# Fused cross-attention and mixture-of-experts block: the mixed context tile's probabilities move to a buffer of their own, and its text part and the denominators' passes are cut so that a step has at most one of them

## What is computed

```python
ctx_img = context[:, :IMG_LEN]      # 257 rows
ctx_txt = context[:, IMG_LEN:]      # 1344 rows
q = rms_norm(linear(x, q_w, q_b), norm_q_w).reshape(B, L, NH, HD)      # L = 512, NH = 16, HD = 32
...
scores = jnp.einsum('bqhd,bkhd->bhqk', q, k) * scale
probs = jax.nn.softmax(scores, axis=-1)
return jnp.einsum('bhqk,bkhd->bqhd', probs, v)
...
img_x = attention(q, k_img, v_img)
txt_x = attention(q, k, v)
out = (txt_x + img_x).reshape(B, L, DIM)
return linear(out, o_w, o_b)
```

## Time and profile before

| | |
|---|---|
| median of 3 runs | 1184.51 us (1183.47 to 1185.18) |
| profiled execution, its own time | 1186.64 us |
| its span in the trace | 1184.9 us |
| granted TensorE clock over the span | 0.996 of full speed |
| busy: TensorE, VectorE, ScalarE, GpSimd | 1113.4, 856.5, 651.0, 201.1 us |
| exponentials (L720), 384 plain ones | 372.3 us, mean 1022 ns |
| additions (L977), 64 and 62 | 146.6 and 142.0 us, mean 2291 and 2290 ns |

### The profile page before, as it was taken

How to read it: one execution, slowest core, us unless ns; L and a number is a source line. 1 busy time by engine, 2 the same in 40 slices (tenths; PEclk the granted TensorE clock), 3 DMA queues, 4 the chain that set the end, 5 groups by cost and what they waited for, 6 DMA issues and landing times. The chain is left out here.

```text
span 1184.9 us, 21824 instructions
## 1 busy us (share of the span) xinstructions
PE 1113.4 (94%) x8948; PEld 414.9 (35%) x8948; DVE 856.5 (72%) x1058; ACT 651.0 (55%) x916; POOL 201.1 (17%) x307
## 2 busy tenths in 40 slices
PE   6899999999999999999998999888999999999996
PEld 2342222344222344422233432222544444333332
DVE  6677889898889988788898878997878942222221
ACT  5558998444999744599964469885221121221221
POOL 1220000143000024300002440001110021333442
PEclk9999999999999999999999999999999999999998
DMA  8852000777300086910009583013823329999742
GB/s 299 193 116 45 2 2 11 165 156 195 74 2 2 11 208 135 207 38 2 2 22 228 134 191 112 2 37 109 343 80 116 116 76 338 357 314 314 220 63 33
DMA packets 142859, 150.15 MB, mean 127 GB/s; under 512 B 108832, under 2 KB 109088, under 8 KB 137760
## 3 DMA queue, kind: packets, MB, share of 16 engines
q1 hardware_dynamic: 135328, 131.57, 38.5%
q0 software_dynamic: 5120, 10.82, 4.7%
q10 hardware_dynamic: 2304, 6.29, 2.1%
HBM read 101.96 MB, written 21.51 MB: 104 GB/s over the span
## 5 line engine op out<-in xcount | busy, mean ns | idle before, releaser
L720 ACT ACTIVATE work<-ps 128x1024 f32<-128x1024 f32 x384 | 372.3, 1022 | 31.3 <-PE ps L1216 15.0
L1222 PE MATMUL ps<-work,vals 128*32 128x512 f32 (+2 forms) x1664 | 220.3, 600 | 3.8 <-DVE nums L965 2.1
L1073 PE MATMUL ps<-wts,work 128*128 128x512 f16 x864 | 194.7, 379 | 11.2 <-DVE work L779 10.9
L1216 PE MATMUL ps<-quer,keys 32*128 32x512 f16 x2496 | 171.9, 377 | 22.7 <-ACT work L720 15.5
L977 DVE TENSOR_TENSOR work<-work 128x2048 f32<-128x2048 f32 x64 | 146.6, 2291 | 6.2 <-ACT work L720 0.5
L977 DVE TENSOR_TENSOR attn<-attn,work 128x2048 f32<-128x2048 f32 x62 | 142.0, 2290 | 5.1
L1073 PEld LDWEIGHTS ps<-wts,work 128*128 128x128 f16 x864 | 83.0, 98 | 118.6 <-issue 19.0
L1878 DVE COPY xgt<-ps 128x320 f32<-128x320 f32 x32 | 15.7, 491 | 137.3 <-PE ps L2046 137.3
L2055 PE MATMUL ps<-wring,xgt 128*80 128x512 f32 x256 | 114.9, 592 | 0.0
L1073 PE MATMUL ps<-wts,hl 128*128 128x512 f16 x432 | 100.5, 384 | 12.9 <-DVE wts L761 7.5
L535 POOL TENSOR_SCALAR small<-small 128x1 f32<-128x1 f32 x68 | 20.1, 295 | 540.2 <-ACT work L630 540.2
(11 more groups left out here) (224 smaller groups left out, 1399.2 us busy)
## 6 DMA issues: line engine op xcount, KB each, us to landing
wring<-in_wx SPq DMA_DIRECT2D x32, 1536.0 KB, 8.5
raw<-in_ctx SPq DMA_DIRECT2D x52, 256.0 KB, 3.2
rb<-sums_inverse ACTq DMA_DIRECT2D x48, 128.0 KB, 4.0
work<-in_x SPq DMA_DIRECT2D x8, 512.0 KB, 4.4
table<-nums SPq DMA_DIRECT2D x16, 256.0 KB, 2.5
work<-in_x SPq DMA_DIRECT2D x12, 256.0 KB, 3.1
x<-work SPq DMA_DIRECT2D x12, 256.0 KB, 2.7
x2t_rows<-nums SPq DMA_DIRECT2D x12, 256.0 KB, 2.6
```

Source lines behind the costliest of these rows:

```text
L720: act.activation(prob[0:rows, s % PROBS, 2 * half:2 * half + 2, :], ps[0:rows, 2 * pair:2 * pair + 2, :], ACT.Exp, scale=SCALE, bias=pad i ...
L1073: mm = pe.matmul(out, lhs(a, c)[:, cols], wts[:, w, z, c * D:(c + 1) * D], start=(k == 0), stop=(k == len(steps) - 1))
L1216: mm = pe.matmul(ps[:, 2 * pair + h % 2, :], k[h * HD:(h + 1) * HD, :], q[h * HD:(h + 1) * HD, :], start=(e == 0), stop=(e == len(terms) - 1))
L1222: return pe.matmul(ps[h * HD:(h + 1) * HD, NUM, :], vals[a:z, ORDER[n], g * P + h * HD:g * P + (h + 1) * HD], prob[a:z, s % PROBS, h, :], ...
```

## The change

The probabilities of the mixed tile get a buffer of their own, `mixp`, 8 KB a partition at the place of `raw`, `hl0` and `rcp`, which rest during attention. The ring `prob` then holds only the 12 other tiles of a group: `place(g, n)` numbers them, `used` gives the count of `a_av` at which a tile's last reader is done, and `chances` picks the buffer. The exponentials of tile 2 wait for the mixed pieces of the group before. In the first group of batches 1 to 3 they wait for `f_chk` instead, because `rcp` lies in the new buffer. The exponentials of n = 3 now wait for the addition of n = 11, those of n = 4 for that of n = 12, and those of n = 5 and 6 for the image sum.

`mixed_text` becomes four pieces of 128 columns at n = 3, 4, 5 and 6 (`MIXED_AT`), `text_part` moves to n = 2, 7, 8 and 9 (`TEXT_AT`), and the image's four pieces become three of 172, 172 and 168 columns at n = 10, 11 and 12 (`image_third`, `IMAGE_CUT`). `first_loads` waits for the last mixed piece of the batch and stands later in SyncE's order, VectorE converts the next batch's first tile after the additions of n = 9 and 10 instead of 6 and 7, and GpSimd's copies into `sel` (which shares the place of `raw`) wait for the last mixed piece too.

```diff
-IMAGE_AT = [5, 10, 11, 12]
+IMAGE_AT = [10, 11, 12]
+IMAGE_CUT = [0, 172, 344, L]
+MIXED_AT = [3, 4, 5, 6]
+TEXT_AT = [2, 7, 8, 9]
...
+        self.mixp = at("mixp", 194 * KB_, [P, 4, L], F32)
...
+        def place(g, n):
+
+            return g * (KT - 1) + (n if n < 2 else n - 1)
+
+        def used(bb, g, n):
+
+            return bb * NG * (KT - 1) + place(g, n) + 1
+
+        def chances(g, n):
+
+            return m.mixp if n == 2 else prob[:, place(g, n) % PROBS, :, :]
...
             def first_loads(bb, b):
-                sp.wait_ge(c_lo, kvn(bb - 1, KT - 2))
+                sp.wait_ge(a_av, used(bb - 1, NG - 1, MIXED_AT[-1]))
+                load_ctx(bb, b, 0)
                 load_ctx(bb, b, 1)
-                sp.wait_ge(c_lo, kvn(bb - 1, KT - 1))
-                load_ctx(bb, b, 0)
...
-                pool.wait_ge(c_lo, kvn(bb, KT - 1))
+                pool.wait_ge(a_av, used(bb, NG - 1, MIXED_AT[-1]))
...
-                    if s >= PROBS:
-                        a = s - PROBS
-                        m = a % KT
-                        act.wait_ge(a_av, step(bb, a + 1 if m == 2 else a))
-                        if m < 2 and bb < B:
-                            act.wait_ge(a_sum, imaged(bb, a // KT))
-                        if m >= 3:
-                            act.wait_ge(a_sum, added(bb, a // KT, max(m - 4, 0)))
+                    if n == 2:
+                        if g > 0:
+                            act.wait_ge(a_av, used(bb, g - 1, MIXED_AT[-1]))
+                        elif 0 < bb < B:
+                            act.wait_ge(f_chk, 2 * bb)
+                    elif place(g, n) >= PROBS:
+                        pg, pn = divmod(place(g, n) - PROBS, KT - 1)
+                        pn = pn if pn < 2 else pn + 1
+                        act.wait_ge(a_av, used(bb, pg, pn))
+                        if pn < 2 and bb < B:
+                            act.wait_ge(a_sum, imaged(bb, pg))
+                        if pn >= 3:
+                            act.wait_ge(a_sum, added(bb, pg, max(pn - 4, 0)))
...
-                            if n == 6:
+                            if n == 9:
                                 ctx_high(bb + 1, 0)
-                            if n == 7:
+                            if n == 10:
                                 ctx_low(bb + 1, 0)
...
-                        mixed_text(s - 1, 0, HALF)
+                        mixed_text(g, 0)
                     else:
+                        if n in MIXED_AT:
+                            mixed_text(g, MIXED_AT.index(n))
...
-                        if g > 0 and 6 <= n < 10:
...
+                    if g > 0 and n in TEXT_AT:
+                        k = TEXT_AT.index(n)
+                        if k == 0:
+                            pe.wait_ge(a_sum, added(bb, g - 1, ADDS - 1))
+                        mm = text_part(g - 1, k * P, (k + 1) * P)
...
-                    if s % KT == 4:
-                        mixed_text(s - 2, HALF, L).then_inc(a_av, 1)
```

More of the change, by code:

```diff
@@ L656, in project @@
                 if bb > 0:
-                    act.wait_ge(a_av, step(bb - 1, STEPS - 2))
+                    act.wait_ge(a_av, used(bb - 1, NG - 1, KT - 2))
                     if b > 0:
@@ L719, in exponentials @@
                         pair = (u + 2) % 3
-                        act.activation(prob[0:rows, s % PROBS, 2 * half:2 * half + 2, :],
+                        act.activation(chances(g, n)[0:rows, 2 * half:2 * half + 2, :],
                                        ps[0:rows, 2 * pair:2 * pair + 2, :], ACT.Exp, scale=SCALE,
@@ L961, in sums_and_results @@
                         dve.wait_ge(a_exp, unit(bb, 2 * s + 1))
-                        cur = fl(prob[:, s % PROBS, :, :])
+                        cur = fl(chances(g, n))
                         if n == KT - 1:
-                            dve.wait_ge(a_av, step(bb, s))
+                            dve.wait_ge(a_av, used(bb, g, n))
                             dve.tensor_copy(nums[:, g, 0, :], ps[:, NUM, :]).then_inc(a_nt, 1)
@@ L1223, in numerator @@
                                      vals[a:z, ORDER[n], g * P + h * HD:g * P + (h + 1) * HD],
-                                     prob[a:z, s % PROBS, h, :], start=first, stop=last)
+                                     chances(g, n)[a:z, h, :], start=first, stop=last)
                 def numerators(s, rows, first, last):
@@ L1233, in image_part, with image_third @@
                         mm = pe.matmul(ps[h * HD:(h + 1) * HD, DEN, a:z], ones[0:rows, 1, s // KT, :],
-                                       prob[0:rows, s % PROBS, h, a:z], start=first, stop=False)
+                                       chances(s // KT, s % KT)[0:rows, h, a:z], start=first, stop=False)
                     return mm
-                def image_quarter(g, k):
+                def image_third(g, k):
+                    a, z = IMAGE_CUT[k], IMAGE_CUT[k + 1]
                     for h in range(4):
-                        pe.matmul(ps[h * HD:(h + 1) * HD, DEN, k * P:(k + 1) * P], ones[:, 1, g, :],
-                                  image[:, h, k * P:(k + 1) * P], start=False, stop=False)
+                        pe.matmul(ps[h * HD:(h + 1) * HD, DEN, a:z], ones[:, 1, g, :], image[:, h, a:z],
+                                  start=False, stop=False)
                 def mixed_image(s):
@@ L1245, in mixed_image, with mixed_text @@
                         pe.matmul(ps[h * HD:(h + 1) * HD, DEN, :], ones[0:SPLIT, 2, g, :],
-                                  prob[0:SPLIT, s % PROBS, h, :], start=(g == 0 and bb < B), stop=False)
+                                  m.mixp[0:SPLIT, h, :], start=(g == 0 and bb < B), stop=False)
                         mm = numerator(s, h, SPLIT, P, False, True)
                     return mm
-                def mixed_text(s, a, z):
-                    g, n = s // KT, s % KT
+                def mixed_text(g, k):
+                    a, z = k * P, (k + 1) * P
                     for h in range(4):
                         pe.matmul(ps[h * HD:(h + 1) * HD, NUM, a:z],
-                                  vals[0:SPLIT, ORDER[n], g * P + h * HD:g * P + (h + 1) * HD],
-                                  prob[0:SPLIT, s % PROBS, h, a:z], start=False, stop=False)
-                        mm = pe.matmul(ps[h * HD:(h + 1) * HD, DEN, a:z], ones[SPLIT:P, 2, g, :],
-                                       prob[SPLIT:P, s % PROBS, h, a:z], start=False, stop=False)
-                    return mm
+                                  vals[0:SPLIT, MIX, g * P + h * HD:g * P + (h + 1) * HD],
+                                  m.mixp[0:SPLIT, h, a:z], start=False, stop=False)
+                        pe.matmul(ps[h * HD:(h + 1) * HD, DEN, a:z], ones[SPLIT:P, 2, g, :],
+                                  m.mixp[SPLIT:P, h, a:z], start=False, stop=False)
                 def text_part(g, a, z, last=False):
@@ L1299, in weighted @@
                                 pe.matmul(ps[h * HD:(h + 1) * HD, DEN, :], ones[:, 0, g, :],
[L1300 to L1307 removed]
+                                          chances(g, n)[:, h, :], start=False, stop=False)
+                    if g > 0 and n in TEXT_AT:
[3 more added lines that the diff above has]
+                        mm = text_part(g - 1, k * P, (k + 1) * P)
+                        if k == QT - 1:
+                            mm.then_inc(a_den, 1)
                 scores(0)
```

20 lines of the change are left out of this document (6 added, 14 removed).

## The result

| | before | changed |
|---|---|---|
| median of 5 runs | 1184.51 us (1182.79 to 1186.86) | 1192.90 us (1191.81 to 1196.31) |
| span of the profiled execution | 1184.9 us | 1191.1 us |

The ratio of the runs is 1.0066 with a 95% interval of 1.0048 to 1.0084, or 5.7 to 9.9 us more. 1185.0 was forecast with a range to 1190.5, so the time lies outside.

A forecast was written before the change was run, and what follows sets the result against it. ScalarE's exponentials, coupled with TensorE's scores, set the pace at 1.96 us a step. First batch -1.5, second and third +0.3 each, last +1.1 gave +0.2, taken as +0.5 on the 1184.51 median: 1185.0 us, range 1180.5 to 1190.5.

The forecast's parts named there:

- the one on the first group: First group, batches 1 to 3 counted from 0: exponentials of n = 2 wait for f_chk, delaying everything behind by 2.33 us.
- +0.2 us: All four batches' attention: the summed change against the profiled execution's 1186.64 us.
- +1.8: First group of each batch after the first: cost 3.29 us for 1.46 us of stops removed.
- 0.39: Mixed piece of 128 columns on TensorE: text piece's 0.34 us plus 0.05 for more matmuls.
- 0.34 each: Last batch, paced by VectorE: its loop gets 0.34 us shorter, three times.
- 0.56 in the forecast: Fourth group of the first batch: gain of 0.56 us, 0.87 paid for 1.43 removed.
- 0.16 + 0.19 + 0.48: Added us in a group's steps: text piece at n = 2, mixed pieces at n = 3 and at n = 4 to 6.
- 0.15 - 0.03: Image thirds at n = 10 to 12 add 0.15 us, hidden at n = 12; two pieces leaving full steps save 0.03.
- +1.8 - 1.0 + 0.4: Last batch: first group's cost, three shorter loops, then late pieces and longer third; summed there to +1.1 us.
- Short passes don't pay: Rival: mixed piece costs 0.59 us, total 1195; decides from 0.43 up; chance 0.23.
- Pieces fit: Rival: mixed piece costs 0.24 us, total 1177; decides from 0.34 down; chance 0.20.
- Something late elsewhere: Rival: GpSimd's copies against the additions, or raw loads, cost 2 to 3 us; total 1187.5; chance 0.10.

The follow-up runs named there:

- e2: Changed kernel plus ten unread matmuls on TensorE in the stop before n = 2 of batches 2 to 4; 1190.77 us, ratio 1.0032 to the kernel before.
- e1: Changed kernel with check_sums moved ahead of the projection's last value copy; 1181.52 us, ratio 0.9969 to the kernel before.
- e5: Kernel before plus only the wait for f_chk at n = 2 in the first group of batches 2 to 4; 1198.48 us, ratio 1.0100.
- e6: e4 with the image's denominators in thirds at n = 10, 11, 12 instead of quarters; 1181.44 us, ratio 0.9962 to the kernel before.
- e4: e1 with the cuts of before: mixed_text whole, image quarters, own buffer kept; 1181.42 us, ratio 0.9956 to the kernel before.
- e7: e4 with the second half of mixed_text moved into step n = 4; 1178.72 us, ratio 0.9940 to the kernel before.
- e8: e7 with GpSimd's eight copies into sel behind the last batch's denominators; 1177.97 us, ratio 0.9934 to the kernel before.
- e9: e2 with four unread matmuls instead of ten; 1190.17 us, ratio 1.0031 to the kernel before.
- e10: The changed kernel once more, unaltered, in one execution; 1196.47 us.

## Why the prediction was wrong, point by point

**The step that failed** is the one on the first group: "That is 2.33 with everything of the stage behind it." The stop itself was right (2.19 idle, and 2.30 by e2 against e1). What was left out is what it does to TensorE. It waits through the stop, 2.65 us by the profile, and the granted clock falls to 0.50 behind it. From the first n = 1 to the reciprocals the forecast was +0.2 us and the profiles give +5.96; two falls of 2.59 are 5.2 of the 5.8 between them. That e2 fills only the idle time and loses the slow stretch, and that e5 has it in the kernel before by the wait alone, shows it. I had looked at the granted clock only as it stood in the kernel before (1.00), and had asked of the new wait which instructions are queued behind it, not which engine would stand idle.

The trace of before held the warning. At the start of its expert part TensorE idles for 3.46 us, and the first products behind that take twice the time of the same ones 3 us later:

```profile
831.01 2.05 PE L1914 MATMUL ps<-rcp,sel 128*128 128x512 f32 x2 [3.46 <-PEq L166]
...
834.22 1.02 PE L1914 MATMUL ps<-rcp,sel 128*128 128x512 f32 x2
```

The granted clock is 0.50 from 831 to 833 there. The other idle stretches of TensorE in that trace, behind its first matmul, are 1.83 us at most, and the granted clock stays at 1.00 behind them. The new stop lies between the two, so those rows alone could have given a rival but not its chance.

The Trainium skill (TensorE: Matmul & The Clock Gate, HAM oscillation — how this bites in real kernels) describes this for a loop that waits for transfers: the waits let the clock fall and each next stretch of work starts slowly. The traces agree, with a semaphore in place of a transfer: 1.00 before the stop, 0.50 behind it. The waits that the Trainium skill shows there are longer, about 3 to 5 us; here 2.65 was enough in eight cases of nine. Either way it would have made a rival with its own price.

**What held.** Without a fall the first group takes 29.37 us, 1.88 above before, for +1.8. A mixed piece takes 0.38 (311.87 to 312.25), for 0.39. In the last batch the third group takes 28.78 us (765.44 to 794.22), 0.30 less than before's 29.08 (760.47 to 789.55), and the second 28.05 for 28.28, 0.23 less, for 0.34 each. Batch 1 gained 1.66 for 1.5, but in part by luck: its groups gave 0, 0.29 and 0.30, and 1.07 came from the fourth group and the projection behind it, for 0.56 in the forecast, a stretch that varies by more than that between kernels which are alike there.

**What was mis-sized.** The steps with mixed pieces and the text piece at n = 2 stop ScalarE five times for 0.19 to 0.20, each step 2.13 us: 17 hundredths above 1.96, 0.87 together for my 0.16 + 0.19 + 0.48 = 0.83. The thirds were too cheap. From 345.06 to 355.07 five steps take 10.01 us; before, eight steps with text pieces take 15.77 (337.99 to 353.76), or 9.86 for five. The n = 2 exponentials to those of n = 3 take 2.02 (330.41 to 332.43) for 1.96. That is 0.21 in place of 0.15 - 0.03, and e6 has 0.20 against e4. I had called the third at n = 12 hidden, and it is not. The rest are the hundredths of full steps that I had rounded away. Together the period is 26.71 for 26.53, about 2 us over all groups. The sum has a slip as well: +1.8 - 1.0 + 0.4 is +1.2 and not +1.1. These are errors within the range; the two falls are what carried the time out of it.

**The rivals.** *Short passes don't pay* would have given the right time for a wrong reason: it wanted a piece at 0.43 or more, and it is 0.38. *Pieces fit* was wrong, each piece costs 0.17 a step. *Something late elsewhere* named GpSimd's copies; they did become four times as long, and cost 0.5 us on VectorE, of which nothing reached TensorE: its last denominators start 0.86 us behind the product before them (822.84 to 823.70), and 0.85 before (818.09 to 818.94). No rival had the clock.

**Where the expected gain went.** The buffer removes two stops, 0.59 in a group. The cuts turn one stop of 0.84 into five of 0.17 and 0.2 for the thirds, which is no gain. The wait for `f_chk` costs 2.3 us in each of three batches, and the clock 2.6 in each that has a full fall.

What stays open: why the stretch from a fourth group's n = 1 to the next batch's first takes anything from 119.5 to 122.5 us and the part behind the reciprocals 364.7 to 368.4 in the twelve profiles, in no order that the edits explain; this is what hides a gain of 1 or 2 us in the totals. Also open is whether e7 and e8 are really faster than e4, and why the same idle time ends in a fall in one execution and not in another.

## What to carry to other kernels

A new wait has two prices: what is queued behind it, and what the clock does to the engine that runs dry meanwhile. If TensorE would idle for as long as here (2.65 us, or even the 1.69 of e9) in a stretch that runs at the full clock, move the work that is waited for (e1 did it by placing 1.5 us of VectorE work in a gap) before cutting anything finer.

Cutting a block to fill the spare time of several steps pays only if what the pieces, each with its change of tile shape, take above the spare time is less in sum than the one stop was. Here pieces of 0.38 us met 0.22 of spare time, and five steps lost 0.87 in place of one stop of 0.84. When a change moves a buffer over another's place, the waits that come with the place belong to its price: here the place, not the buffer, made it a loss.

## What the runs showed of the hardware that I had not expected

- The granted clock of TensorE fell to 0.50 behind an idle stretch of 2.65 us between stretches of dense work, and was back at 1.00 after 6.8 us (after 3.4 in e10's third batch). With 3.46 us idle it fell in the kernel before, with 1.69 in one of three cases of e9, with 0.39 in none of e2, and the same instructions in the same batch fell in one execution and not in the other.
- Scores of 0.83 us and numerators of 1.07 take 1.47 and up to 1.94 us there (e5's numerators), and ScalarE waits up to 1.35 us for a step.
- GpSimd's eight copies take 9.28 us beside VectorE's additions of two operands, 2.41 beside other work and 1.95 beside the reciprocals, and the additions beside them take 2.43 in place of 2.29 and start 2.53 apart in place of 2.40 (over all six in e7, some of them not beside the copies, the mean is 2.51).
